# Macaron block with attention: key tiles scored in groups of four, values loaded on a semaphore of their own

## The chip, the cores and the metric

The kernel runs on one core of one Trainium2 chip. The metric is the time of one execution on the device in microseconds (us); lower is better. Engines are named as in the profile: PE is TensorE, PEld its weight loads, DVE is VectorE, ACT is ScalarE, POOL is GpSimd, SP is SyncE, which here only issues DMAs.

## The reference: what is computed

```python
x = x + 0.5 * ffn(layernorm(x), up, down, up_scale, down_scale, output_scale)
x = x + attention(layernorm(x), w_q, w_k, w_v, w_o)
x = x + 0.5 * ffn(layernorm(x), up, down, up_scale, down_scale, output_scale)

def attention(x, w_q, w_k, w_v, w_o):       # x: (2, 2048, 512), 16 heads of 32
    q, k, v = heads(x @ w_q.T), heads(x @ w_k.T), heads(x @ w_v.T)
    probs = softmax(q @ k.T / sqrt(32))
    return merge(probs @ v) @ w_o.T

def ffn(x, ...):                            # hidden size 2048, weights by their sign
    h = relu(x @ sign(up).T * up_scale)
    return h @ sign(down).T * down_scale * output_scale
```

Everything is float32. The attention part is what the change touches: two batches of 16 heads, 32 heads in all, each with 2048 queries and 2048 keys.

## The kernel before

The program has four stages: the first feed-forward part, the projections to queries, keys and values (stored in DRAM, queries and keys each as a rounded high part and a low part), the attention over 32 heads, and the output projection together with the second feed-forward part. Every engine has its instructions written out by hand in one order, and semaphores tie the engines together.

A head has 16 key tiles of 128 keys (`KT`) and four chunks of 512 queries (`QC`). One key tile with one chunk is called a **unit** here; a head has 64. For a unit, PE makes a block of scores, keys by queries, in one matmul with 98 rows (`scores`, L899 to L904: high and low parts stacked, and two rows that carry the negated maximum of each query). ACT takes the exponential of it into SBUF (L891). Three PSUM banks (`SR`) rotate for the scores, so the scores of a unit wait for the exponential three units earlier.

The maximum of each query has to be known before its scores are made, so beside each score block PE makes a block of queries by keys for a head later in time (`maxima`, L906 to L908; it runs four tiles ahead, `LEAD`), and DVE reduces that block to a maximum for each query (L836). Four banks (`MR`) rotate for these blocks. So PE's maxima of a unit wait until DVE has read the block four before it (`bank_free`, L962 to L974). In the last of the 32 heads, and the last four tiles of the one before, there are no maxima to make.

When all 64 maxima blocks of the next head are reduced, the **turn** follows: DVE negates them (L848), PE transposes the 128 by 16 result (L926), DVE splits it into a high and a low part (L854, L856), and SP writes both as two rows of the queries' tile (L769). The next head's first scores wait for these rows (`neg_loaded`, L979).

The probabilities of a key tile are multiplied by the values in `out_tile` (L928 to L943): four matmuls with 32 columns, one for each chunk, which use different columns of the array and run beside each other. POOL and DMAs with accumulation add the probabilities up for the softmax's denominator; PE finishes that with a matmul by ones (`sums`, L945 to L960) once a head. Eight tiles of probabilities (`PR`) rotate.

What sets PE's order in a head is `tensor_group` (L976 to L1003). A group is `G` = 2 key tiles. PE runs the eight units of the group, scores and maxima in turn, and then the outputs of the group before: `out_tile` for its two tiles. So a head has eight groups. The turn's transpose comes behind the group of tiles 12 and 13, the sums of the head before behind that of tiles 6 and 7, and ACT copies the head before's output out of its bank in the group of tiles 2 and 3 (L893).

SP, at the head's start, waits until PE has made all outputs of the head before (`head_free`, L772), and then issues in this order: the six loads of queries and keys for the head after next and the load of its values (L761, L763, seven DMAs on one semaphore), the four stores of the finished head (L297), the two moves of its sums (L302, L306), the two rows of maxima (L769) and the store of the inverse (L311).

Of the kernel before, what the change touches and what calls it, by code (L numbers as in the profile page):

```python
# [650 lines left out]

NB = 3
KQ, KM = 3 * HD, 3 * HD + 2
LEAD, G = 4, 2
NG = KT // G
PR = 8
SR, MR = 3, 4
UNITS = KT * QC
AHEAD = LEAD * QC
SUMS_AFTER = 3  # L660
SUMS_AT, TURN_AT = QC * G * (SUMS_AFTER + 1), QC * 7 * G
SLOTS = UNITS + 2
CHAINS = 2
PER = 7 * 16
TURN = KT - LEAD + 1
NEG = 3


def sums_after(H):

    return SUMS_AFTER if H < NH - 1 else SUMS_AFTER - 1


def chains_joined(H):
# [47 lines left out]
class Attention:  # L722
# [3 lines left out]
    def __init__(self, c, qk_parts, v_scr, head_out, ident, ones_sum):  # L726
        self.nc, self.qk_parts, self.v_scr, self.head_out, self.ident, self.ones_sum = c.nc, qk_parts, v_scr, head_out, ident, ones_sum
        self.q_st = [c.sb(f"att_q{i}", at, [P, SEQ], F32R) for i, at in enumerate((OUT_AT, HID_LO_AT, X0_AT))]
        self.k_st = [c.sb(f"att_k{i}", at, [P, SEQ], F32R) for i, at in enumerate((HID_HI_AT, INV_B_AT, RAW_AT))]
        self.v_st = [c.sb(f"att_v{i}", at, [P, KT, HD]) for i, at in enumerate((HID_AT + 2, HID_AT, INV_AT))]  # L730
        self.prob = [c.sb(f"att_p{i}", BIG_AT + 8 * i, [P, SEQ]) for i in range(PR)]
        self.acc = [c.sb(f"att_acc{i}", at, [P, SEQ]) for i, at in enumerate((CENT_AT, HI1_AT))]
        self.dma_acc = [[c.sb(f"att_dma_acc{i}_{x}", at, [P, SEQ]) for x, at in enumerate(ats)]
                        for i, ats in enumerate(((WORK_AT, SUM_AT), (LO1_AT, X1_AT)))]
        self.row_max = [c.sb(f"att_row_max{i}", HEAD_AT + 4 + 0.25 * i, [P, KT, QC]) for i in range(2)]
        self.neg_max = c.sb("att_neg_max", HEAD_AT + 4.5, [P, KT])
        self.neg_hi, self.neg_lo = c.sb("att_neg_hi", HEAD_AT + 5, [KT, P], F32R), c.sb("att_neg_lo", HEAD_AT + 5.5, [KT, P], F32R)
        self.m_ps, self.s_ps, self.o_ps = c.bank[0:4], c.bank[4:7], c.bank[7]
        self.loaded = [c.sem(f"att_loaded{i}") for i in range(NB)]
# [15 lines left out]


    def load(self, sp, X):
        b, row, col = X % NB, X % HEADS * HD, X // HEADS * SEQ
        for which, st in ((0, self.q_st[b]), (1, self.k_st[b])):
            for i, part in enumerate(((0, 0, 1), (0, 1, 0))[which]):  # L760
                sp.dma_start(f32(st[i * HD:(i + 1) * HD, :]),  # L761
                             self.qk_parts[which][part][row:row + HD, col:col + SEQ]).then_inc(self.loaded[b], 16)
        sp.dma_start(self.v_st[b][:], self.v_scr[col:col + SEQ, row:row + HD].rearrange("(t p) d -> p t d", p=P)  # L763
                     ).then_inc(self.loaded[b], 16)

    def max_rows(self, sp, H):
        for r, rows in enumerate((self.neg_hi, self.neg_lo)):
# [1 line left out]
            sp.dma_start(f32(self.q_st[H % NB][KQ + r:KQ + r + 1, :].rearrange("o (t p) -> o t p", p=P)),  # L769
                         f32(rows[:])).then_inc(self.neg_loaded, 16)  # L770

    def head_free(self, sp, H):  # L772

        sp.wait_ge(self.s_ready, UNITS * H)
        sp.wait_ge(self.p_used, KT * H)


# [79 lines left out]

    def vector_tile(self, dve, H, kt):
        T = H + 1 + (kt + LEAD) // KT
        for q in range(QC):  # L860
            p = QC * kt + q
            if T < NH:
                self.reduce_block(dve, UNITS * (H + 1) + AHEAD + p, self.m_ps[m_bank(H, slot(p))], T % 2, (kt + LEAD) % KT, q)
            if kt == TURN - 1 and q == 0 and H + 1 < NH:
                self.negate(dve, H + 1)
        if kt == TURN and H + 1 < NH:
            self.rows_out(dve, H + 1, self.turn_bank(H))
        if H > 0 and kt == (14 if H < NH - 1 else 12):
            self.head_out.invert(dve, H - 1)

# [12 lines left out]

    def scalar_tile(self, act, H, kt):
        self.tile_free(act, H, kt)
        if H > 0 and kt == G * (sums_after(H) + 1):
            act.wait_ge(self.t_ready, H)
            self.head_out.copy_sums(act, H - 1, self.sums_bank(H - 1))
        for q in range(QC):
            act.wait_ge(self.s_ready, UNITS * H + QC * kt + q + 1)  # L890
            self.nc.scalar.activation(self.prob[kt % PR][:, q * CH:(q + 1) * CH], self.s_ps[(UNITS * H + kt * QC + q) % SR][:], ACT.Exp,  # L891
                                      scale=SCALE).then_inc(self.exp_done, 1)
            if q == 1 and H > 0 and kt == G:  # L893
                act.wait_ge(self.p_used, KT * H)
                self.head_out.copy_out(act, H - 1, self.o_ps)

# [30 lines left out]

    def out_tile(self, pe, H, kt):  # L928
        pe.wait_ge(self.exp_done, UNITS * H + QC * (kt + 1))
        if kt == 0 and H > 0:  # L930
            pe.wait_ge(self.head_out.out_copied, H)
        for q in range(QC):
# [43 lines left out]
    def tensor_group(self, pe, H, u, beside=None):  # L976

        if u == 0:
            pe.wait_ge(self.neg_loaded, 32 * (H + 1))  # L979
            pe.wait_ge(self.ones_set, min(H + 1, NB))  # L980
        for kt in range(G * u, G * u + G):
            T = H + 1 + (kt + LEAD) // KT
            if kt == KT - LEAD and T < NH:
                pe.wait_ge(self.loaded[T % NB], PER * (T // NB + 1))
            for q in range(QC):
                self.scores(pe, H, kt, q)
                if T < NH:
                    at = slot(QC * kt + q)
                    self.bank_free(pe, H, at)
                    self.maxima(self.m_ps[m_bank(H, at)], T, (kt + LEAD) % KT, q)  # L990
                if beside:
                    beside(QC * (kt - G * u) + q)
        if G * u <= TURN < G * u + G and H + 1 < NH:
            self.bank_free(pe, H, TURN_SLOT)
            self.transpose_max(pe, H + 1, self.turn_bank(H))
        for kt in range(G * u - G, G * u):
            if kt >= 0:
                self.out_tile(pe, H, kt)
            elif H > 0:
                self.out_tile(pe, H - 1, KT + kt)  # L1000
        if u == sums_after(H) and H > 0:
            self.bank_free(pe, H, SUMS_SLOT)
            self.sums(pe, H - 1)  # L1003
# [8 lines left out]
FIRST_TURN = (NCH - 1, 6)  # L1012
FOUR_FROM = FIRST_FROM[NCH - 1, 0]


def macaron_kernel(nc, xT, w_qT, w_kT, w_vT, w_oT, upT, downT, up_scale, down_scale, output_scale, outT):
    ctx = ExitStack()
    with ctx:
# [40 lines left out]
        with nc.Block() as block:  # L1059
            @block.sync  # L1060
            def _(sp):
# [23 lines left out]
                for n in range(NCH):  # L1085
# [3 lines left out]
                    for t in range(NT):  # L1089
                        qkv.store(sp, n, t)  # L1090
                        if n == 4 and t == 2:
                            qkv.all_stored(sp, 4)
                            sp.wait_ge(att.ones_set, 2)
                            att.load(sp, 0)
                        if n == 4 and t == 6:
                            att.load(sp, 1)
                        if (n, t) == FIRST_TURN:
                            att.max_rows(sp, 0)
                qkv.all_stored(sp, NCH)

                for H in range(NH):
                    if H > 0:
                        att.head_free(sp, H)
                    if H + 2 < NH:
                        att.load(sp, H + 2)
                    if H == 0:
                        sp.dma_start(wo_raw[:], w_oT).then_inc(wo_loaded, 16)
                    if H == LAST - 1:
# [196 lines left out]
            def _(pe):  # L1305
# [23 lines left out]
                pe.wait_ge(qkv.qk_read, 8 * NCH)  # L1329
                pe.wait_ge(qkv.v_read, 4 * NCH)  # L1330
                for H in range(NH):
                    for u in range(NG):
                        def beside(i):
                            t = u + 1 if H == LAST else 0
                            first = (H, u, i) == (LAST - 1, NG - 1, 0)
                            if first:
# [4 lines left out]
                            if (H, u) == (LAST - 1, NG - 1) or (H == LAST and u < 3):  # L1341
                                oproj.product(pe, 0, t, range(STEPS * i // 8, STEPS * (i + 1) // 8))
# [6 lines left out]
                for kt in range(KT - G, KT):  # L1349
                    att.out_tile(pe, LAST, kt)  # L1350
                att.sums(pe, LAST)

# [41 lines left out]
```

## Time and profile before

| what | value |
|---|---|
| time of the kernel before, median of 3 runs | 2979.45 us (2978.91 to 2981.06) |
| the profiled execution's own time | 2976.84 us |
| its span on the core | 2975.0 us |
| mean granted TensorE clock | 0.994 |
| PE busy | 2898.6 us, 97% of the span |
| DVE busy | 2051.4 us, 69% |
| ACT busy | 1603.5 us, 54% |
| POOL busy | 1383.1 us, 46% |
| attention: first and last score matmul | 817.9 and 2404.6 us |

The profiled execution lies inside the program's usual time: 1.84 us lie around its span, and it is 2.61 us below the median of the three runs. The attention takes 1587 us of the span, more than half. The times of the rows below are microseconds from the start of the span.

### The profile page before, as it was taken

What the parts mean: (1) busy time and instruction counts of PE and PEld (TensorE: products, weight loads), DVE (VectorE), ACT (ScalarE), POOL (GpSimd) and SP (SyncE); (2) the same over time, 40 slices, a digit from 0 to 9 for tenths busy, and PEclk for the clock granted to TensorE, in tenths of its full rate; (3) what the DMA queues carried; (4) which work ended last, traced back from release to release, by engine and by line L of the source; (5) the groups of instructions that cost most, each with busy time, mean ns of one, the idle gap of its engine ahead of it and who ended that gap; (6) DMA issues with size and microseconds to landing.
All of it is one profiled execution on the core that took longest, in us unless ns stands there. A gap on an engine that the chain in (4) does not pass through costs nothing.

```text
span 2975.0 us, 38468 instructions
## 1 busy us (share of the span) xinstructions
PE 2898.6 (97%) x14528; PEld 1939.1 (65%) x14528; DVE 2051.4 (69%) x3050; ACT 1603.5 (54%) x2851; POOL 1383.1 (46%) x522
## 2 busy tenths in 40 slices
PE   6999998999999999999999999999999899999999
PEld 5888887887755555555555555555555457888887
DVE  5555555767787787878787878788888355555553
ACT  5444434332276666666666666666666553343333
POOL 0000000000089898988898889898888720000000
PEclk9999999999999999999999999999999999999999
DMA  4110002555389999998999999999898872222200
GB/s 154 59 57 29 29 29 62 199 192 177 124 219 205 220 209 224 203 231 198 228 203 233 200 229 202 229 204 229 204 229 207 220 196 69 57 57 57 57 29 29
DMA packets 189275, 459.97 MB, mean 155 GB/s; under 512 B 90273, under 2 KB 91297, under 8 KB 148769
## 3 DMA queue, kind: packets, MB, share of 16 engines
q0 software_dynamic: 36720, 267.40, 39.0%
q1 hardware_dynamic: 152368, 190.11, 22.6%
q8 instruction: 114, 1.87, 0.3%
q14 instruction: 73, 0.59, 0.1%
HBM read 121.91 MB, written 67.63 MB: 64 GB/s over the span
## 4 chain that ended last, share of the span: by engine, by line
PE 88%; DVE 4%; DMA 3%; ACT 3%; POOL 1%; issue 1%; SPq 0%; ACTq 0%; DVEq 0%; POOLq 0%
PE bank L903 16%; PE bank L511 16%; PE bank L530 15%; PE bank L934 15%; PE bank L907 14%; PE bank L642 8%; PE bank L382 3%; ACT att_p L891 2%; DMA att_q<-att_neg_lo 1%; DVE att_row_max L836 1%; PE bank L958 1%; PE bank L950 1%; DVE norm_inv L109 1%; DVE norm_work L119 1%; POOL att_acc L792 1%
## 5 line engine op out<-in xcount | busy, mean ns | idle before, releaser
L836 DVE TENSOR_REDUCE att_row_max<-bank 128x1 f32<-128x512 f32 x2048 | 1255.2, 681 | 318.0 <-PE bank L907 318.0
L891 ACT ACTIVATE att_p<-bank 128x512 f32<-128x512 f32 x2048 | 1035.5, 627 | 414.3 <-PE bank L903 408.5
L792 POOL TENSOR_TENSOR att_acc<-att_acc,att_p 128x2048 f32<-128x2048 f32 x217 | 1066.6, 4915 | 32.8 <-ACT att_p L891 28.2
L903 PE MATMUL bank<-att_q,att_k 98*128 98x512 f32 x2048 | 848.5, 415 | 18.2 <-ACT att_p L891 11.2
L907 PE MATMUL bank<-att_k,att_q 96*128 96x512 f32 x2048 | 808.1, 396 | 10.8 <-DVE att_row_max L836 10.6
L903 PEld LDWEIGHTS bank<-att_q,att_k 98*128 98x128 f32 x2048 | 384.4, 188 | 396.7 <-issue 202.4
L934 PE MATMUL bank<-att_p,att_v 128*32 128x512 f32 x4096 | 497.1, 603 | 0.0
L443 DVE TENSOR_TENSOR ffn_hid_lo<-ffn_hid,ffn_hid_hi 128x512 fp32r<-128x512 f32 x256 | 176.0, 688 | 420.8 <-ACT ffn_hid_hi L486 402.5
L483 ACT ACTIVATE ffn_hid<-bank,up_s 128x512 f32<-128x512 f32 x256 | 176.1, 688 | 488.0 <-PE bank L511 487.2
L907 PEld LDWEIGHTS bank<-att_k,att_q 96*128 96x128 f32 x2048 | 389.6, 190 | 60.6 <-DVE att_row_max L836 13.3
L511 PE MATMUL bank<-hi,ffn_up_w 128*128 128x512 f32 x1024 | 401.0, 392 | 13.6 <-DVE lo L123 13.6
L530 PE MATMUL bank<-ffn_hid_hi,ffn_down_w 128*128 128x512 f32 x1024 | 399.6, 390 | 1.9 <-DVE ffn_hid_lo L443 1.9
L511 PE MATMUL bank<-lo,ffn_up_w 128*128 128x512 f32 x1024 | 400.7, 391 | 0.0
L530 PE MATMUL bank<-ffn_hid_lo,ffn_down_w 128*128 128x512 f32 x1024 | 399.7, 390 | 0.0
L780 POOL MEMSET att_k<- 2x2048 f32 x3 | 5.4, 1805 | 814.8 <-PE bank L530 501.7
L807 POOL DMA_DIRECT2D att_dma_acc<-att_p x161 | 203.8, 1266 | 139.4 <-DMA att_dma_acc<-att_p 97.8
L934 PEld LDWEIGHTS bank<-att_p,att_v 128*32 128x32 f32 x4096 | 107.5, 109 | 242.8 <-ACT att_p L891 158.5
L511 PEld LDWEIGHTS bank<-hi,ffn_up_w 128*128 128x128 f32 x1024 | 193.6, 189 | 56.1 <-issue 15.2
L530 PEld LDWEIGHTS bank<-ffn_hid_hi,ffn_down_w 128*128 128x128 f32 x1024 | 192.7, 188 | 42.9 <-DVE ffn_hid_lo L443 2.4
L511 PEld LDWEIGHTS bank<-lo,ffn_up_w 128*128 128x128 f32 x1024 | 193.6, 189 | 40.8
L530 PEld LDWEIGHTS bank<-ffn_hid_lo,ffn_down_w 128*128 128x128 f32 x1024 | 192.7, 188 | 40.5
L486 ACT ACTIVATE ffn_hid_hi<-bank,up_s 128x512 fp32r<-128x512 f32 x256 | 174.6, 682 | 0.0
(104 smaller groups left out, 2236.8 us busy)
## 6 DMA issues: line engine op xcount, KB each, us to landing
att_dma_acc<-att_p POOLq DMA_DIRECT2D x225, 1024.0 KB, 8.9
att_dma_acc<-att_dma_acc POOLq DMA_DIRECT2D x30, 1024.0 KB, 12.6
x<-x_after_ffn SPq DMA_DIRECT2D x16, 1024.0 KB, 7.6
att_q<-q_hi SPq DMA_DIRECT2D x64, 256.0 KB, 4.0
att_k<-k_hi SPq DMA_DIRECT2D x64, 256.0 KB, 10.0
x_after_ffn<-x_out SPq DMA_DIRECT2D x8, 1024.0 KB, 9.4
q_hi<-qkv_o_hi SPq DMA_DIRECT2D x32, 256.0 KB, 2.0
q_lo<-qkv_o_lo SPq DMA_DIRECT2D x32, 256.0 KB, 2.4
```

Source lines behind the costliest of these rows:

```text
L443: nc.vector.tensor_tensor(self.hid_lo[:, ht % RING, :], self.hid[:, ht % RAW, :], f32(self.hid_hi[:, ht % RING, :]), ALU.subtract).then_in ...
L483: nc.scalar.activation(self.hid[:, ht % RAW, :], self.up_ps[ht % 2][:], ACT.Relu, scale=self.vecs["up"][:, ht:ht + 1])
L511: ins = nc.tensor.matmul(self.up_ps[ht % 2][:], signs.up[:, ht // 4, dt, ht % 4 * P:(ht % 4 + 1) * P], part[N % 2][:, dt, :], start=(dt == ...
L530: ins = nc.tensor.matmul(self.down_ps[dt][:], signs.down[:, h, dt * P:(dt + 1) * P], part[:, h % RING, :], start=(h == 0 and i == 0), stop ...
L642: ins = self.nc.tensor.matmul(self.out_ps[t % QR][:], left, right, start=(dt == 0 and (a, b) == (0, 0)), stop=(dt == DT - 1 and (a, b) == ...
L792: self.nc.gpsimd.tensor_tensor(self.acc[H % 2][:], a[:], self.prob[kt % PR][:], ALU.add).then_inc(self.summed, 1)
L807: self.nc.gpsimd.dma_start(into[:], self.prob[kt % PR][:], accum_op=ALU.add).then_inc(self.dma_summed[x], 16)
L836: self.nc.vector.tensor_reduce(self.row_max[odd][:, qt, q:q + 1], m[:], axis=AX.X, op=ALU.max).then_inc(self.m_read, 1)
L891: self.nc.scalar.activation(self.prob[kt % PR][:, q * CH:(q + 1) * CH], self.s_ps[(UNITS * H + kt * QC + q) % SR][:], ACT.Exp, scale=SCALE ...
L903: self.nc.tensor.matmul(self.s_ps[i % SR][:], self.k_st[H % NB][0:KM, kt * P:(kt + 1) * P], self.q_st[H % NB][0:KM, q * CH:(q + 1) * CH], ...
L907: self.nc.tensor.matmul(m[:], self.q_st[T % NB][0:KQ, qt * P:(qt + 1) * P], self.k_st[T % NB][0:KQ, q * CH:(q + 1) * CH], start=True, stop ...
L934: ins = self.nc.tensor.matmul(self.o_ps[rows, :], self.v_st[H % NB][:, kt, :], self.prob[kt % PR][:, q * CH:(q + 1) * CH], start=(kt == 0) ...
```

## The change

Tiles are grouped by four instead of by two in all heads but the last (`GROUPS`), which keeps pairs (`PAIRS`). So PE makes 16 units of scores and maxima in a row and then the outputs of the four tiles of the group before. The sums come behind the group of tiles 4 to 7. The turn comes behind the outputs that follow the group of tiles 8 to 11, since with a lead of four tiles the next head's maxima are complete there; DVE negates and splits ahead of its reductions of tile 12. ACT copies the head before's output in tile 4. Values have a semaphore of their own, `v_loaded`, which the first output of a head waits for. SP loads queries and keys as soon as all scores of the head before are made, and values once all its outputs are made.

```diff
-LEAD, G = 4, 2
-NG = KT // G
+LEAD = 4
+GROUPS = tuple(tuple(range(kt, kt + 4)) for kt in range(0, KT, 4))
+PAIRS = tuple((kt, kt + 1) for kt in range(0, KT, 2))
+SUMS_GROUP, TURN_GROUP = 1, 2
-SUMS_AT, TURN_AT = QC * G * (SUMS_AFTER + 1), QC * 7 * G
+SUMS_AT, TURN_AT = QC * GROUPS[SUMS_GROUP + 1][0], QC * (KT - LEAD)
-PER = 7 * 16
+PER = 6 * 16
+def groups(H):
+    return GROUPS if H < NH - 1 else PAIRS
...
+    def load_values(self, sp, X):
+        b, row, col = X % NB, X % HEADS * HD, X // HEADS * SEQ
         sp.dma_start(self.v_st[b][:], self.v_scr[col:col + SEQ, row:row + HD].rearrange("(t p) d -> p t d", p=P)
-                     ).then_inc(self.loaded[b], 16)
+                     ).then_inc(self.v_loaded[b], 16)
...
-    def head_free(self, sp, H):
+    def scores_made(self, sp, H):
         sp.wait_ge(self.s_ready, UNITS * H)
+    def outputs_made(self, sp, H):
         sp.wait_ge(self.p_used, KT * H)
...
     def vector_tile(self, dve, H, kt):
+        if kt == KT - LEAD and H + 1 < NH:
+            self.negate(dve, H + 1)
+            self.rows_out(dve, H + 1, self.turn_bank(H))
...
-            if kt == TURN - 1 and q == 0 and H + 1 < NH:
-                self.negate(dve, H + 1)
-        if kt == TURN and H + 1 < NH:
-            self.rows_out(dve, H + 1, self.turn_bank(H))
...
-            if q == 1 and H > 0 and kt == G:
+            if q == 1 and H > 0 and kt == groups(H)[1][0]:
                 act.wait_ge(self.p_used, KT * H)
                 self.head_out.copy_out(act, H - 1, self.o_ps)
...
     def out_tile(self, pe, H, kt):
         pe.wait_ge(self.exp_done, UNITS * H + QC * (kt + 1))
+        if kt == 0:
+            pe.wait_ge(self.v_loaded[H % NB], 16 * (H // NB + 1))
...
-        for kt in range(G * u, G * u + G):
+        first = groups(H)[u][0]
+        for kt in groups(H)[u]:
...
-        if G * u <= TURN < G * u + G and H + 1 < NH:
+        if u > 0:
+            for kt in groups(H)[u - 1]:
+                self.out_tile(pe, H, kt)
+        elif H > 0:
+            for kt in groups(H - 1)[-1]:
+                self.out_tile(pe, H - 1, kt)
+        if u == TURN_GROUP and H + 1 < NH:
             self.bank_free(pe, H, TURN_SLOT)
             self.transpose_max(pe, H + 1, self.turn_bank(H))
-        for kt in range(G * u - G, G * u):
-            if kt >= 0:
-                self.out_tile(pe, H, kt)
-            elif H > 0:
-                self.out_tile(pe, H - 1, KT + kt)
...
                 for H in range(NH):
                     if H > 0:
-                        att.head_free(sp, H)
+                        att.scores_made(sp, H)
                     if H + 2 < NH:
                         att.load(sp, H + 2)
+                    if H > 0:
+                        att.outputs_made(sp, H)
+                    if H + 2 < NH:
+                        att.load_values(sp, H + 2)
```

How the instructions stand, at the places on which the prediction rests. First PE, at the end of the first stretch of scores (L903, and L914 in the changed kernel) and maxima (L907, and L918) of the attention's first head; L934 and L947 are the outputs. Before, 32 such matmuls, those of 16 units, run ahead of the first outputs, since the first group of the first head has no outputs behind it:

```order
L903 MATMUL bank<-att_q_84,att_k_87 128x512 [waits att_exp_done]
L907 MATMUL bank<-att_k_88,att_q_85 128x512 [waits att_m_read]
L934 MATMUL bank<-att_p_93,att_v_90 32x512 [waits att_exp_done]
L934 MATMUL bank<-att_p_93,att_v_90 32x512 x3
L934 MATMUL bank<-att_p_94,att_v_90 32x512 [waits att_exp_done]
L934 MATMUL bank<-att_p_94,att_v_90 32x512 x3
L903 MATMUL bank<-att_q_84,att_k_87 128x512 [waits att_exp_done]
```

And now at the same place, ahead of which 32 units run in this first head (16 in all later groups):

```order
L914 MATMUL bank<-att_q_84,att_k_87 128x512 [waits att_exp_done]
L918 MATMUL bank<-att_k_88,att_q_85 128x512 [waits att_m_read]
L947 MATMUL bank<-att_p_93,att_v_90 32x512 [waits att_v_loaded0,att_exp_done]
L947 MATMUL bank<-att_p_93,att_v_90 32x512 x3
L947 MATMUL bank<-att_p_94,att_v_90 32x512 [waits att_exp_done]
L947 MATMUL bank<-att_p_94,att_v_90 32x512 x3
L947 MATMUL bank<-att_p_95,att_v_90 32x512 [waits att_exp_done]
L947 MATMUL bank<-att_p_95,att_v_90 32x512 x3
L947 MATMUL bank<-att_p_96,att_v_90 32x512 [waits att_exp_done]
L947 MATMUL bank<-att_p_96,att_v_90 32x512 x3
L914 MATMUL bank<-att_q_84,att_k_87 128x512 [waits att_exp_done]
```

The outputs of four tiles now stand together, and the waits on `att_m_read` (DVE's reading of a maxima block) and `att_exp_done` are the same ones on twice as long a stretch.

DVE over the end of one head in the middle of the attention, before; `att_row_max` is where the reductions go, `head_inv_t` the inverse of the head before's sums:

```order
L836 TENSOR_REDUCE att_row_max_107<-bank 128x1 [waits att_m_ready]
L848 TENSOR_REDUCE att_neg_max<-att_row_max_108 128x16 [waits att_neg_pe,att_m_read]
L836 TENSOR_REDUCE att_row_max_107<-bank 128x1 [waits att_m_ready] x7
L854 CAST att_neg_hi<-bank 16x128 [waits att_neg_loaded,att_neg_pe]
L856 TENSOR_TENSOR att_neg_lo<-bank,att_neg_hi 16x128 [waits att_neg_dve]
L836 TENSOR_REDUCE att_row_max_107<-bank 128x1 [waits att_m_ready] x4
L318 RECIPROCAL head_inv_t<-head_tot_t 128x16 [waits head_inv_stored,head_sums_moved]
```

And now:

```order
L848 TENSOR_REDUCE att_row_max_108<-bank 128x1 [waits att_m_ready] x52
L860 TENSOR_REDUCE att_neg_max<-att_row_max_108 128x16 [waits att_neg_pe,att_m_read]
L866 CAST att_neg_hi<-bank 16x128 [waits att_neg_loaded,att_neg_pe]
L868 TENSOR_TENSOR att_neg_lo<-bank,att_neg_hi 16x128 [waits att_neg_dve]
L848 TENSOR_REDUCE att_row_max_107<-bank 128x1 [waits att_m_ready] x12
L318 RECIPROCAL head_inv_t<-head_tot_t 128x16 [waits head_inv_stored,head_sums_moved]
```

The negation and the split have moved ahead of the reductions of tiles 12 to 15, and DVE now waits there for PE's transpose with no reduction in between.

SP at the start of a head, before:

```order
L761 DMA att_q_84<-q_hi 32x2048 [waits att_p_used,att_s_ready]
L761 DMA att_q_84<-q_hi 32x2048
L761 DMA att_q_84<-q_lo 32x2048
L761 DMA att_k_87<-k_hi 32x2048
L761 DMA att_k_87<-k_lo 32x2048
L761 DMA att_k_87<-k_hi 32x2048
L763 DMA att_v_90<-v_rows 128x16x32
L297 DMA attention_out<-head_raw 32x512 [waits head_out_copied]
```

And now:

```order
L767 DMA att_q_84<-q_hi 32x2048 [waits att_s_ready]
L767 DMA att_q_84<-q_hi 32x2048
L767 DMA att_q_84<-q_lo 32x2048
L767 DMA att_k_87<-k_hi 32x2048
L767 DMA att_k_87<-k_lo 32x2048
L767 DMA att_k_87<-k_hi 32x2048
L772 DMA att_v_90<-v_rows 128x16x32 [waits att_p_used]
L297 DMA attention_out<-head_raw 32x512 [waits head_out_copied]
```

The order of the DMAs is the same; the wait for the outputs (`att_p_used`) has moved from the first load to the load of the values.

## Rows read from the trace of the kernel before

**Rows 1.** The page: the chain that ended last, shares of the span by engine

```profile
PE 88%; DVE 4%; DMA 3%; ACT 3%; POOL 1%; issue 1%; SPq 0%; ACTq 0%; DVEq 0%; POOLq 0%
```

**Rows 2.** Busy time in 200 us of the attention (us, busy of each engine, clock, DMA)

```profile
1420.00:1620.00 200.00, 199.03 (x1116) 108.17 (x1116) 162.06 (x278) 135.00 (x269) 175.28 (x65) 1.00 0.93 216
```

**Rows 3.** The chain in order of time, one head (start us, us, what)

```profile
1551.25 1.85 PE bank L934 x16
...
1557.05 1.85 PE bank L934 x16
...
1563.28 1.85 PE bank L934 x16
...
1576.73 0.86 PE bank L950 x8
1577.59 0.86 PE bank L958 x8
...
1594.11 0.28 PE bank L926
...
1600.18 1.85 PE bank L934 x16
```

**Rows 4.** PE's timeline over one group (start, us, line, what [idle before <-releaser])

```profile
1503.85 0.50 PE L903 MATMUL bank<-att_q,att_k 98*128 98x512 f32 x1 [0.32 <-DMA att_q<-att_neg_lo]
1504.19 0.40 PE L907 MATMUL bank<-att_k,att_q 96*128 96x512 f32 x1
...
1507.47 0.40 PE L907 MATMUL bank<-att_k,att_q 96*128 96x512 f32 x1
1507.80 1.92 PE L934 MATMUL bank<-att_p,att_v 128*32 128x512 f32 x16
1509.65 0.50 PE L903 MATMUL bank<-att_q,att_k 98*128 98x512 f32 x1
```

**Rows 5.** DVE's timeline, same head

```profile
1504.63 4.88 DVE L836 TENSOR_REDUCE att_row_max<-bank 128x1 f32<-128x512 f32 x8 [1.21 <-PE bank L907]
...
1550.41 0.24 DVE L318 RECIPROCAL head_inv_t<-head_tot_t 128x16 f32<-128x16 f32 x1
```

**Rows 6.** The page: the reductions (xcount | busy, mean ns | idle before)

```profile
L836 DVE TENSOR_REDUCE att_row_max<-bank 128x1 f32<-128x512 f32 x2048 | 1255.2, 681 | 318.0 <-PE bank L907 318.0
```

**Rows 7.** The timeline of the first head's first 16 units

```profile
817.51 10.96 DVE L836 TENSOR_REDUCE att_row_max<-bank 128x1 f32<-128x512 f32 x18 [0.57 <-PE bank L907]
...
817.98 0.47 PE L903 MATMUL bank<-att_q,att_k 98*128 98x512 f32 x1 [0.27 <-issue]
...
819.19 7.95 ACT L891 ACTIVATE att_p<-bank 128x512 f32<-128x512 f32 x16
...
826.13 0.19 PEld L907 LDWEIGHTS bank<-att_k,att_q 96*128 96x128 f32 x1 [0.23 <-DVE att_row_max L836]
...
826.56 1.92 PE L934 MATMUL bank<-att_p,att_v 128*32 128x512 f32 x16
```

**Rows 8.** PE's waits from 820 to 2405 us (total, times, longest)

```profile
PE bank L903 <- DMA att_q<-att_neg_lo: 2.9, 5, 1.0
```

**Rows 9.** SP's timeline (start, us, what)

```profile
1512.52 0.42 SPq L763 DMA_DIRECT2D att_v<-v_rows  x1
1512.99 15.29 SPq L297 DMA_DIRECT2D attention_out<-head_raw  x4
1530.33 0.55 SPq L302 DMA_DIRECT2D prob_sums<-head_total  x1
1535.70 0.34 SPq L306 DMA_DIRECT2D head_tot_t<-prob_sums  x1
...
1547.70 1.38 SPq L769 DMA_DIRECT2D att_q<-att_neg_lo  x1
```

**Rows 10.** ACT's timeline in the second to last head

```profile
2326.42 1.91 ACT L366 ACTIVATE hi<-op_raw 128x2048 fp32r<-128x2048 f32 x1 [4.59 <-POOL op_raw L353]
```

**Rows 11.** The chain in order of time, between the last two heads

```profile
2353.99 1.12 SPq L344
```

More of the change, by code:

```diff
@@ L659 @@
 AHEAD = LEAD * QC
-SUMS_AFTER = 3
-SUMS_AT, TURN_AT = QC * G * (SUMS_AFTER + 1), QC * 7 * G
+SUMS_AT, TURN_AT = QC * GROUPS[SUMS_GROUP + 1][0], QC * (KT - LEAD)
 SLOTS = UNITS + 2
 CHAINS = 2
-PER = 7 * 16
-TURN = KT - LEAD + 1
+PER = 6 * 16
 NEG = 3
+def groups(H):
+    return GROUPS if H < NH - 1 else PAIRS
 def sums_after(H):
-    return SUMS_AFTER if H < NH - 1 else SUMS_AFTER - 1
+    return SUMS_GROUP if H < NH - 1 else 2
 def chains_joined(H):
@@ L738, in __init__ @@
         self.m_ps, self.s_ps, self.o_ps = c.bank[0:4], c.bank[4:7], c.bank[7]
-        self.loaded = [c.sem(f"att_loaded{i}") for i in range(NB)]
+        self.loaded, self.v_loaded = [c.sem(f"att_loaded{i}") for i in range(NB)], [c.sem(f"att_v_loaded{i}") for i in range(NB)]
         self.ones_set = c.sem("att_ones_set")
@@ L885, in scalar_tile @@
         self.tile_free(act, H, kt)
-        if H > 0 and kt == G * (sums_after(H) + 1):
+        if H > 0 and kt == groups(H)[sums_after(H) + 1][0]:
             act.wait_ge(self.t_ready, H)
@@ L991, in tensor_group @@
                 if beside:
-                    beside(QC * (kt - G * u) + q)
-        if G * u <= TURN < G * u + G and H + 1 < NH:
+                    beside(QC * (kt - first) + q)
+        if u > 0:
[5 more added lines that the diff above has]
+        if u == TURN_GROUP and H + 1 < NH:
             self.bank_free(pe, H, TURN_SLOT)
             self.transpose_max(pe, H + 1, self.turn_bank(H))
-        for kt in range(G * u - G, G * u):
-            if kt >= 0:
-                self.out_tile(pe, H, kt)
-            elif H > 0:
-                self.out_tile(pe, H - 1, KT + kt)
         if u == sums_after(H) and H > 0:
@@ L1012 @@
 FIRST_TURN = (NCH - 1, 6)
+FILL_FROM = QC * len(GROUPS[-1]) - 8
 FOUR_FROM = FIRST_FROM[NCH - 1, 0]
@@ L1094, in _ @@
                             att.load(sp, 0)
+                            att.load_values(sp, 0)
                         if n == 4 and t == 6:
                             att.load(sp, 1)
+                            att.load_values(sp, 1)
                         if (n, t) == FIRST_TURN:
@@ L1331, in _ @@
                 for H in range(NH):
-                    for u in range(NG):
+                    for u in range(len(groups(H))):
                         def beside(i):
                             t = u + 1 if H == LAST else 0
-                            first = (H, u, i) == (LAST - 1, NG - 1, 0)
-                            if first:
+                            ahead = (H, u) == (LAST - 1, len(GROUPS) - 1) and i >= FILL_FROM
+                            if ahead and i == FILL_FROM:
                                 pe.wait_ge(att.m_read, UNITS * NH)
@@ L1340, in beside @@
                                 pe.wait_ge(att.neg_dve, NEG * NH)
-                            if (H, u) == (LAST - 1, NG - 1) or (H == LAST and u < 3):
-                                oproj.product(pe, 0, t, range(STEPS * i // 8, STEPS * (i + 1) // 8))
+                            if ahead or (H == LAST and u < 3):
+                                j = i - FILL_FROM if ahead else i
+                                oproj.product(pe, 0, t, range(STEPS * j // 8, STEPS * (j + 1) // 8))
                             if (H, u, i) == (LAST, 3, 7):
@@ L1348, in _ @@
                         att.tensor_group(pe, H, u, beside)
-                for kt in range(KT - G, KT):
+                for kt in PAIRS[-1]:
                     att.out_tile(pe, LAST, kt)
```

## The prediction

> **What bounds the kernel now.** I read the chain by engine first: 88% of it is PE [rows 1]. Then a stretch in the middle of the attention: in 200 us PE is busy 199.03, at the full clock, while DVE has 162.06, ACT 135.00 and POOL 175.28 [rows 2]. So a head lasts as long as PE's instructions, and the question is what PE's own order costs. The chain over one head gives that: from the outputs of one head's first group to those of the next, 1551.25 to 1600.18, are 48.93 us [rows 3]. A plain group of two tiles lasts 5.80 (1551.25 to 1557.05). The head has eight of them, 46.40; ACT's copy of the finished head makes one of them 6.23 (to 1563.28), 0.43 more; the sums are twice 0.86; the transpose of the turn is 0.28. That makes 48.83, and 0.10 is left over.
>
> Inside a group, count from its first score, 1503.85 [rows 4]. The first maxima follow at 0.34, the eighth at 3.62 (1507.47), so 14 steps of 0.234 lie between, and a unit of scores and maxima takes 0.468. The outputs start 0.33 later, at 3.95, and 16 of them take 1.85, until 5.80.
>
> DVE needs longer for a unit than PE. It starts 0.78 after the first score (1504.63) and takes 4.88 for eight reductions [rows 5]; one lasts 0.68 [rows 6], so they start (4.88 - 0.68) / 7 = 0.60 apart. In each unit DVE falls back 0.13, and it catches up while PE makes outputs, which need nothing of it. That is the heart of this case.
>
> **Groups of four.** Maxima of unit n take the bank of unit n - 4, so they start at the earliest when DVE has finished that one: 0.78 + 0.60 (n - 4) + 0.68, and a handover. For n = 7, the last of a group now, this is 3.26 against the 3.62 at which PE is there anyway: no wait. With 16 units PE would be at the last maxima at 0.34 + 30 x 0.234 = 7.36, but DVE has finished unit 11 only at 0.78 + 11 x 0.60 + 0.68 = 8.06.
>
> The trace of before holds this stretch once: the first head's first group has no outputs behind it, so 16 units run in a row there [rows 7]. DVE's 18 reductions are two left over and these 16, (10.96 - 0.68) / 17 = 0.605 apart. The one for unit 11 is the 14th and ends at 817.51 + 13 x 0.605 + 0.68 = 826.05; the weight load of the last maxima comes at 826.13 and is put down to DVE. The handover is 0.08, and the outputs come 0.43 behind it, not 0.33. From the first score to the outputs it is 826.56 - 817.98 = 8.58; my reckoning gives 8.06 + 0.08 + 0.43 = 8.57. ACT paces the start of this stretch, (7.95 - 0.60) / 15 = 0.49 for a unit, but not its end.
>
> So a group of four takes 8.57 + 32 outputs at 1.85 / 16, 3.70, together 12.27, against 2 x 5.80 = 11.60: 0.67 more. Without DVE it would be 7.36 + 0.33 + 3.70 = 11.39, 0.21 less than now, since one change from outputs to scores and back is saved (0.34 and 0.33 where a step is 0.234) [rows 4].
>
> The Trainium skill (VectorE: DVE Perf Modes, the section on the TRN2 errata) gives a VectorE instruction that reads PSUM 120 cycles and one for each element at 0.96 GHz, which for 512 is 0.66 us. That is near the 0.68 of one instruction, but the starts here are 0.60 apart; taken as the pace it would put the last maxima at 8.78 and the forecast some 75 us higher. The measurement decides.
>
> **The head's other pieces.** ACT's copy moves to tile 4, the start of the second group. It still holds up a few scores, but DVE has started by then and its pace sets the group's end: even with the copy's 0.49, ACT finishes unit 12 at about 0.6 + 12 x 0.49 + 0.49 + 0.6 = 7.6, before 8.06. So its 0.43 goes, and the 0.10 too. Sums and transpose stay, 1.72 and 0.28; the negation is done while PE makes the 3.70 of outputs ahead of the transpose, and the split (two instructions of 0.28 or so) fits into the 0.78 that DVE stands anyway. The head becomes 4 x 12.27 + 2.00 = 51.08, so 51.08 - 48.93 = 2.15 more. If the copy isn't hidden it is 2.58; if the hold is 0.1 less in each group, 1.75.
>
> 29 heads (the second to the thirtieth): 29 x 2.15 = +62.4. The first head: 32 units now run in a row, 0.78 + 27 x 0.60 + 0.68 + 0.08 + 0.43 = 18.2, then 3.7, then 12.27 and 12.55: 46.7; before 8.58 + 1.85 + 6 x 5.80 + 0.28 = 45.5. That is +1.2. The last head keeps pairs.
>
> The thirty-first head has a hold of its own: ACT stands 4.59 until POOL has scaled the first chunk of the output projection, at 2326.42 [rows 10]. POOL's place from the head's start stays, so the first two groups' extra goes into that wait. But PE comes out of it with four tiles' outputs more still to make (tiles 4 to 7 stand behind the third group now), 3.7, less about 0.5 for the changes between outputs and scores saved after it: +3.2. From there the end follows, since SP's loads for the projection wait for the last outputs of this head, at 2353.99 [rows 11]. Bounds 0 and 5.
>
> **The turn.** The transpose now has 0.28 + 8.57 + 3.70 = 12.6 us ahead of the next head's first score; before it was 1594.11 to 1600.18 + 1.85, 7.9 [rows 3]. The rows of maxima were late by up to 1.0, in all 2.9 us of PE [rows 8]; at one head it is the 0.32 in rows 4. SP's issue at 1547.70 [rows 9] comes 43.9 into the head; now it can be at about 40 of 51. That wait goes: -2.9, at most.
>
> **Loads.** Queries and keys are issued about 6 to 10 us sooner, values about 3.6 later (12.3 into the head, where the outputs end, against 1512.52 - 1503.85 = 8.7). Neither was waited for; both have a head or more: nothing. What is queued behind the values on SP is the point: the four stores took 15.29 behind them, then the sums move out at 1530.33, 26.5 into the head, and in again at 1535.70, 31.9 [rows 9]. DVE wants them at 1550.41, 46.6 [rows 5]. Now the stores end about 28.1 into the head, so the sums come 1.7 later, at 33.6, and DVE wants them at 46.8: 13 us for a small transfer. Nothing, but it is rival three. POOL and the DMA engines (0.93 busy [rows 2]) get the same work in a longer head.
>
> **The sum.** 62.4 + 1.2 + 3.2 - 2.9 = +63.9 on the profiled execution's 2976.84 gives 3040.7; the median of the runs lies 2.6 above that execution, so 3043.3.
>
> **Rivals.** *Fewer switches win (faster).* If DVE didn't hold PE in the second half of a group, a head would be 4 x 11.39 + 0.43 + 2.00 + 0.10 = 48.1, 0.85 less, and with the turn's 2.9 the time would be 2979.45 - 30 x 0.85 - 2.9 = 2951. For it: DVE has 318 us of idle time in its reductions [rows 6], so on average it keeps up. Against it: it is held to four banks, and rows 7 show the wait. It decides if DVE's pace came to 0.53 or less. The Trainium skill (TensorEngine Tiling (Array Packing), Key Properties) says that changing the tiling mode drains the TensorE, and outputs with 32 columns are another mode than scores; the trace agrees, at 0.1 us a switch. By that rule alone this change is a gain. Chance 4%.
>
> *The hold is half as large*, because what saves PE elsewhere in a long stretch doesn't show in the first head, where ACT paced the start: a group of 11.39 + 0.44 = 11.83, a head 4 x 11.83 + 2.00 = 49.32, +0.39, time 2979.45 + 29 x 0.39 + 1.2 + 3.2 - 2.9 = 2992. Against it: the formula doesn't use ACT's pace and meets 8.58. Chance 8%; and 2% that it all cancels.
>
> *SP's queue becomes a wait (much slower).* If the sums of the head before land more than 13 us after their issue, DVE stands at L318 with tile 15's reductions behind it, and PE behind those. Each us late costs 29; 2 us late gives about 3100. For it: DMAs are dense and the stores already took 15 us. Against it: 13 us are left. Chance 8%.
>
> **How the numbers follow.** The forecast has 78%. Its own range is 0.4 us for a head either way, the two bounds of a head above, 12 in all, and 0 to 5 for the tail: 3028 to 3057. Towards the half-sized hold I go down to 3024, and to 3058 above; it leaves out about 20%. What a measurement of this kernel can tell from no change is 0.2%, 6 us. Faster 4%, same 2%, slower 94%.
>
> **What would show it.** Right: a head of 51 us in the chain; weight loads of the maxima (now L918) held by DVE late in each group, about 0.8 us a group; DVE's reductions in runs of 16 of about 9.7; no wait for the rows of maxima; ACT's copy costing PE nothing by the group's end. Wrong: groups of 11.4 (rival one), or DVE idle at L318 (rival three). A head of 51 with another total would mean the tail is mis-sized.

## The result and the profile after

| | before | changed |
|---|---|---|
| median of 4 runs | 2979.18 us (2977.14 to 2981.06) | 3011.73 us (3009.84 to 3016.62) |
| ratio to before, 95% interval | | 1.0108 (1.0096 to 1.0120) |
| span of the profiled execution | 2975.0 us | 3008.0 us |
| one head in the middle | 48.93 us | 50.15 us |

The change makes the kernel slower by 1.1%, 32.6 us. I had forecast slower, by 64. The direction and its mechanism were right, the loss that I forecast was twice the one measured, and the time lies under my range.

The chain of the changed kernel in order of time over one head (start us, us, what), which answers to [rows 3]:

```profile
1502.19 3.57 PE bank L947 x32
1505.76 0.21 PE bank L937
...
1514.33 3.57 PE bank L947 x32
...
1526.42 3.57 PE bank L947 x32
...
1538.53 3.57 PE bank L947 x32
1542.10 0.86 PE bank L963 x8
1542.96 0.86 PE bank L971 x8
...
1552.34 3.57 PE bank L947 x32
```

From 1502.19 to 1552.34 are 50.15 us. The outputs of four tiles take 3.57, not twice 1.85. A plain group's scores run from 1517.90 (1514.33 + 3.57) to 1526.42, 8.52. The group with the transpose (L937) lasts from 1505.76 to 1514.33, 8.57: the transpose costs 0.04 or so, where it stood in the chain with 0.28 before [rows 3].

PE and its weight loads near the end of a group of four (timeline, [idle before <-releaser]):

```profile
1550.64 0.19 PEld L918 LDWEIGHTS bank<-att_k,att_q 96*128 96x128 f32 x1 [0.30 <-DVE att_row_max L848]
1550.65 0.50 PE L918 MATMUL bank<-att_k,att_q 96*128 96x512 f32 x1
1550.75 0.19 PEld L914 LDWEIGHTS bank<-att_q,att_k 98*128 98x128 f32 x1
1550.98 0.39 PE L914 MATMUL bank<-att_q,att_k 98*128 98x512 f32 x1
1551.24 0.19 PEld L918 LDWEIGHTS bank<-att_k,att_q 96*128 96x128 f32 x1 [0.30 <-DVE att_row_max L848]
...
1551.84 0.19 PEld L918 LDWEIGHTS bank<-att_k,att_q 96*128 96x128 f32 x1 [0.30 <-DVE att_row_max L848]
...
1552.27 0.16 PEld L947 LDWEIGHTS bank<-att_p,att_v 128*32 128x32 f32 x8 [0.24 <-ACT att_p L902]
```

Each maxima block's weight load is released by DVE, 0.60 apart: that is DVE's pace, not PE's 0.47. PE itself has no gap in these rows: the next scores start 0.33 behind the held maxima (1550.98), where a step was 0.234 before, and still inside its 0.50. So the hold shows in PEld's waits and not in PE's busy time. DVE, for the same kernel, now reduces 16 blocks without a gap and then stands:

```profile
1518.60 9.66 DVE L848 TENSOR_REDUCE att_row_max<-bank 128x1 f32<-128x512 f32 x16 [2.33 <-PE bank L918]
1530.70 9.66 DVE L848 TENSOR_REDUCE att_row_max<-bank 128x1 f32<-128x512 f32 x16 [2.44 <-PE bank L918]
```

And the waits of the attention (us in total, times, longest). The first was forecast; before, DVE held a weight load of a maxima block once in the whole attention, the one at 826.13 in [rows 7]. The last, the sign of rival three, came once and was short. The rows of maxima, waited for in [rows 8], are in the list no more:

```profile
PEld bank L918 <- DVE att_row_max L848: 161.6, 579, 0.3
...
DVE head_inv_t L318 <- DMA head_tot_t<-prob_sums: 0.2, 1, 0.2
```

579 is close to 30 heads with four groups of five held loads.

### The profile page after: what moved, and what is told of

Its sections match the earlier page's. It is cut to its first block, busy times and chain, and to the rows that moved or that the text cites. A ratio compares the mean times of both kernels' runs of the same rounds, so it can differ in the third digit from the quotient of the medians.

```text
span 3008.0 us, 38440 instructions
## 1 busy us (share of the span) xinstructions
PE 2938.1 (98%) x14528; PEld 1910.1 (64%) x14528; DVE 2043.4 (68%) x3050; ACT 1615.0 (54%) x2851; POOL 1378.6 (46%) x522
## 4 chain that ended last, share of the span: by engine, by line
PE 92%; DVE 3%; ACT 3%; DMA 1%; issue 1%; POOL 0%; ACTq 0%; SPq 0%; DVEq 0%; POOLq 0%
PE bank L918 17%; PE bank L914 16%; PE bank L511 15%; PE bank L947 15%; PE bank L530 15%; PE bank L642 7%; PE bank L382 3%; ACT att_p L902 2%; PE bank L971 1%; PE bank L963 1%; DMA att_dma_acc<-att_p 1%; DVE norm_inv L109 1%; ACT head_raw L286 0%; DVE norm_work L119 0%; PE bank L176 0%
## 5 line engine op out<-in xcount | busy, mean ns | idle before, releaser
L848 DVE TENSOR_REDUCE att_row_max<-bank 128x1 f32<-128x512 f32 x2048 | 1240.6, 677 | 305.0 <-PE bank L918 305.0
L902 ACT ACTIVATE att_p<-bank 128x512 f32<-128x512 f32 x2048 | 1047.1, 654 | 383.9 <-PE bank L914 370.9
L804 POOL TENSOR_TENSOR att_acc<-att_acc,att_p 128x2048 f32<-128x2048 f32 x217 | 1022.6, 4712 | 220.8 <-ACT att_p L902 216.5
L918 PE MATMUL bank<-att_k,att_q 96*128 96x512 f32 x2048 | 876.0, 429 | 11.0 <-DVE att_row_max L848 11.0
L914 PE MATMUL bank<-att_q,att_k 98*128 98x512 f32 x2048 | 842.4, 413 | 15.5 <-ACT att_p L902 11.7
L914 PEld LDWEIGHTS bank<-att_q,att_k 98*128 98x128 f32 x2048 | 385.5, 188 | 274.1 <-ACT att_p L902 130.8
L918 PEld LDWEIGHTS bank<-att_k,att_q 96*128 96x128 f32 x2048 | 387.2, 189 | 212.4 <-DVE att_row_max L848 175.1
L947 PE MATMUL bank<-att_p,att_v 128*32 128x512 f32 x4096 | 473.8, 602 | 0.0
L947 PEld LDWEIGHTS bank<-att_p,att_v 128*32 128x32 f32 x4096 | 120.6, 110 | 265.5 <-issue 208.1
L819 POOL DMA_DIRECT2D att_dma_acc<-att_p x161 | 160.1, 994 | 18.5 <-DMA att_dma_acc<-att_p 13.1
```

Of the source, the lines that this page charges most:

```text
L804: self.nc.gpsimd.tensor_tensor(self.acc[H % 2][:], a[:], self.prob[kt % PR][:], ALU.add).then_inc(self.summed, 1)
L848: self.nc.vector.tensor_reduce(self.row_max[odd][:, qt, q:q + 1], m[:], axis=AX.X, op=ALU.max).then_inc(self.m_read, 1)
L914: self.nc.tensor.matmul(self.s_ps[i % SR][:], self.k_st[H % NB][0:KM, kt * P:(kt + 1) * P], self.q_st[H % NB][0:KM, q * CH:(q + 1) * CH], ...
L918: self.nc.tensor.matmul(m[:], self.q_st[T % NB][0:KQ, qt * P:(qt + 1) * P], self.k_st[T % NB][0:KQ, q * CH:(q + 1) * CH], start=True, stop ...
L947: ins = self.nc.tensor.matmul(self.o_ps[rows, :], self.v_st[H % NB][:, kt, :], self.prob[kt % PR][:, q * CH:(q + 1) * CH], start=(kt == 0) ...
```

## The experiments

All ratios are to the kernel before, run on the same chip; the medians of before were 2977.4 to 2980.5, by the chip, so two rows are compared by their ratios. The halved reductions leave out half of each block of maxima, so those two kernels are no candidates. "A head" is the distance of two heads' first scores in the middle of the attention.

| kernel | median us | ratio, 95% interval | a head, us |
|---|---|---|---|
| before | 2979 | 1 | 48.93 |
| changed | 3011.73 | 1.0108 (1.0096 to 1.0120) | 50.15 |
| groups of four, halved reductions | 2944.15 | 0.9886 (0.9865 to 0.9908) | 47.88 |
| before, halved reductions | 2966.04 | 0.9966 (0.9953 to 0.9980) | 48.76 |
| pairs with the rest of the change | 2980.04 | 1.0000 (0.9991 to 1.0009) | 48.98 |
| groups of four, loads as before | 3032.69 | 1.0186 (1.0171 to 1.0202) | 50.1 to 55.0 |
| groups of four, copy first | 3012.60 | 1.0106 (1.0091 to 1.0121) | 50.17 |
| before, copy first | 2971.07 | 0.9963 (0.9951 to 0.9975) | 48.6 |
| groups of 3, 3, 2, 2, 2, 2, 2 | 2981.88 | 1.0004 (0.9996 to 1.0013) | 49.10 |
| before, transpose behind the outputs | 2972.83 | 0.9983 (0.9974 to 0.9993) | 48.65 |
| pairs, rest of the change, copy first | 2965.21 | 0.9948 (0.9936 to 0.9960) | 48.65 |
| the same, transpose between scores | 2965.71 | 0.9959 (0.9946 to 0.9972) | 48.59 |
| the same, transpose behind tiles 12 and 13's group | 2958.87 | 0.9931 (0.9917 to 0.9944) | 48.29 |

**Is it DVE that holds a group of four?** Two kernels with DVE's work halved, one in fours and one in pairs:

```diff
-self.nc.vector.tensor_reduce(self.row_max[odd][:, qt, q:q + 1], m[:], axis=AX.X, op=ALU.max)
+self.nc.vector.tensor_reduce(self.row_max[odd][:, qt, q:q + 1], m[:, 0:CH // 2], axis=AX.X, op=ALU.max)
-                                      scale=SCALE)
+                                      scale=SCALE * 0.1)
```

> The changed kernel, but DVE's reductions (L848) read only the first 256 of each maxima block's 512 columns, and the exponential's argument is scaled by a further 0.1 so that it stays finite; half of each row of the maxima is left out. Theory (DVE's pace holds PE in the second half of a group of four): with reductions some 0.33 us apart nothing holds, a group is 7.36 + 0.33 + 3.57 = 11.26 instead of 12.10, ACT's copy costs its 0.43 again, so a head is 4 x 11.26 + 1.72 + 0.03 + 0.43 = 47.2 to 47.5 us instead of 50.14, and the time about 3012 - 30 x 2.8 = 2928 (2920 to 2938). Rival (a group of four is held by something else, ACT's exponentials or PE's own weight loads): the head stays at 49.5 to 50.1 and the time over 2995.

> The kernel before with the same halved reductions and the same scale. Theory: in groups of two DVE never held PE, so the head stays at 48.9 and the time at 2979 within 4 us. Rival: if DVE bounds the kernel before as well, by the average, it falls by more than 10 us.

The chain of the first, one head from 1503.79 to 1551.66:

```profile
1503.79 3.57 PE bank L947 x32
1507.36 0.86 PE bank L963 x8
1508.21 0.86 PE bank L971 x8
...
1517.02 3.57 PE bank L947 x32
1520.59 0.21 PE bank L937
...
1528.40 3.57 PE bank L947 x32
...
1539.78 3.57 PE bank L947 x32
1544.98 0.49 ACT head_raw L286
...
1551.66 3.57 PE bank L947 x32
```

A plain group now lasts 1539.78 - 1528.40 = 11.38 instead of 12.10, and the group with ACT's copy 11.88, so the copy costs its 0.5 again. The head falls from 50.15 to 47.88. It is 0.4 to 0.7 above what I expected, and the time lies 6 us above my range: ACT's exponentials, 0.49 apart, hold the scores where DVE did. Still, the rival's 49.5 to 50.1 is ruled out: it was DVE that held the group.

Pairs fall by 0.17 a head, where I expected nothing, and by 13 us in all. About 3 us of the 13 lie ahead of the attention, in the first reductions, and some in the rows of maxima, which were late less. The 0.17 is at the transpose. In the kernel before, its weight load waits for DVE once in every head, 30 times in all:

```profile
1594.11 0.09 PEld L926 LDWEIGHTS bank<-ident,att_neg_max 128*16 128x16 f32 x1 [0.41 <-DVE att_row_max L836]
```

With halved reductions this wait is gone, and the group with the transpose lasts 1537.34 - 1531.43 = 5.91, 0.11 more than a plain one:

```profile
1531.43 1.85 PE bank L934 x16
...
1537.34 1.85 PE bank L934 x16
...
1543.14 1.85 PE bank L934 x16
```

So of the 0.28 before, only 0.11 is the transpose; 0.17 is a wait for DVE. DVE's pace costs groups of four 2.3 us a head and pairs 0.17. Without it, fours would beat pairs by 0.88. That this is so close to the 0.85 of my first rival is in part luck: its outputs and its transpose were too dear, and it had no hold by ACT.

**Is it the group size alone?**

```diff
-GROUPS = tuple(tuple(range(kt, kt + 4)) for kt in range(0, KT, 4))
-SUMS_GROUP, TURN_GROUP = 1, 2
+GROUPS = PAIRS
+SUMS_GROUP, TURN_GROUP = 3, 5
```

> The changed kernel with groups of two in every head, and all else of the change: the loads' new order, the values' own semaphore, the turn's transpose behind the outputs that follow tiles 10 and 11. Theory: the group size alone makes the change slower; here the transpose costs 0.03 to 0.2 instead of 0.28 (DVE's negation is just not ready when the outputs end) and no head waits for its rows of maxima: 30 x 0.1 to 0.25 plus 3, so 2969 to 2974. Rival (the new order of loads or of the turn costs something): 2979 or more.

Time and head are those of before. So the group size carries all of the loss. The gain that I expected, 5 to 10 us, isn't there; the timeline shows a part of why:

```profile
1542.43 0.22 DVE L860 TENSOR_REDUCE att_neg_max<-att_row_max 128x16 f32<-128x64 f32 x1
1542.76 0.09 PEld L937 LDWEIGHTS bank<-ident,att_neg_max 128*16 128x16 f32 x1 [1.05 <-DVE att_row_max L848]
1542.79 0.27 PE L937 MATMUL bank<-ident,att_neg_max 128*16 128x128 f32 x1 [0.18 <-DVE att_neg_max L860]
```

In pairs the outputs are over before DVE has negated, and PE waits for it at every turn; the group with the turn lasts 0.34 more than a plain one, against 0.30 before. (The 0.37 in later expectations is this 0.34.) In fours the 3.57 of outputs cover the negation. The second head takes back another 1.7 us (52.32 between its first scores and the third's, against 50.66 before); I didn't take that apart.

**What are the loads worth?** Groups of four, with the order of SP as before:

```diff
                         att.scores_made(sp, H)
+                        att.outputs_made(sp, H)
                     if H + 2 < NH:
                         att.load(sp, H + 2)
-                    if H > 0:
-                        att.outputs_made(sp, H)
```

> The changed kernel with SP waiting for scores and outputs of the head before ahead of all seven loads, as before; groups of four stay. Theory: the loads' order isn't on the path; 3012 within 4 us. Rival (the early loads of queries and keys delay other transfers, or gain something): a difference of more than 6 us.

The theory fell: 21 us slower. My third rival happens here, in another form: I had feared that the sums land more than 13 us after their issue; here they take 5.7 (965.35 to 971.07), and the issue itself is late. SP's timeline and DVE's at one of the two slowest heads:

```profile
935.68 0.44 SPq L772 DMA_DIRECT2D att_v<-v_rows  x1
936.16 23.50 SPq L297 DMA_DIRECT2D attention_out<-head_raw  x4
959.70 1.21 SPq L302 DMA_DIRECT2D prob_sums<-head_total  x1
...
965.35 0.33 SPq L306 DMA_DIRECT2D head_tot_t<-prob_sums  x1
```

```profile
955.32 7.25 DVE L848 TENSOR_REDUCE att_row_max<-bank 128x1 f32<-128x512 f32 x12
971.07 0.25 DVE L318 RECIPROCAL head_inv_t<-head_tot_t 128x16 f32<-128x16 f32 x1 [8.51 <-DMA head_tot_t<-prob_sums]
971.24 5.62 DVE L848 TENSOR_REDUCE att_row_max<-bank 128x1 f32<-128x512 f32 x9
```

All seven loads and then the four stores stand in SP's queue, and the stores take 23.50 us to issue. The sums come too late, DVE stands 8.51 at the inverse with reductions behind it, and PE stands behind those. At some twenty other heads DVE's wait is 1.5 to 3.4. The rows of maxima stand behind the sums in SP's queue as well, and at four heads PE waits for them. In the whole attention:

```profile
DVE head_inv_t L318 <- DMA head_tot_t<-prob_sums: 67.7, 22, 8.6
...
PE bank L914 <- DMA att_q<-att_neg_lo: 12.5, 4, 4.8
```

In the changed kernel, with queries and keys issued ahead and the values by themselves, the stores of a head in the middle take 7.07 (they took 15.29 in [rows 9]), and the sums go out before they are late:

```profile
1530.06 0.38 SPq L772 DMA_DIRECT2D att_v<-v_rows  x1
1532.14 7.07 SPq L297 DMA_DIRECT2D attention_out<-head_raw  x4
1544.64 0.55 SPq L302 DMA_DIRECT2D prob_sums<-head_total  x1
```

So the change has two parts that belong together: groups of four delay the point at which all of a head's outputs are made, and with the old order of loads that would cost 21 us more. In pairs all the rest of the change together, loads and turn, is worth nothing in time; no run parts the two, though the stores take less there too (3.6 to 5.1 a head).

**Is ACT's copy hidden in fours, and what is it worth in pairs?**

```diff
+        if H > 0 and kt == groups(H)[1][0]:
+            act.wait_ge(self.p_used, KT * H)
+            self.head_out.copy_out(act, H - 1, self.o_ps)
         for q in range(QC):
...
-            if q == 1 and H > 0 and kt == groups(H)[1][0]:
-                act.wait_ge(self.p_used, KT * H)
-                self.head_out.copy_out(act, H - 1, self.o_ps)
```

> The changed kernel with ACT's copy of the finished head's output ahead of the first exponential of tile 4 instead of behind the second. In groups of four I took the copy to be hidden by DVE's pace. If so, this changes nothing: 3012 within 4 us, head 50.1. Rival (the copy still costs PE about 0.4 a head): about 12 us less.

> The kernel before with ACT's copy ahead of the first exponential of tile 2, where ACT stands idle for 1.8 us, instead of behind the second. In groups of two the copy costs PE 0.43 a head; here it should cost 0.05 to 0.15: 30 x 0.3 to 0.38 less, 2966 to 2971. Rival (the wait for the last outputs comes too late, and the exponentials start later by the copy's whole length): no change or slower.

Both as expected, the second at the upper edge of its range. In fours nothing changes, since DVE's pace sets the group's end. In pairs a head falls by 0.33 and the time by 0.4%: the copy now lies in ACT's idle time.

**Does the formula hold for another size?**

```diff
-GROUPS = tuple(tuple(range(kt, kt + 4)) for kt in range(0, KT, 4))
-SUMS_GROUP, TURN_GROUP = 1, 2
+GROUPS = ((0, 1, 2), (3, 4, 5), (6, 7)) + tuple((kt, kt + 1) for kt in range(8, KT, 2))
+SUMS_GROUP, TURN_GROUP = 2, 4
```

> The changed kernel with groups of 3, 3, 2, 2, 2, 2, 2 tiles in all heads but the last. The formula for the hold gives a group of three 0.78 + 7 x 0.60 + 0.68 + 0.08 = 5.74 at its last maxima, against 5.49 without a hold, and the whole group 5.74 + 0.43 + 2.71 = 8.88. Without a hold it would be 8.53. So the first two groups take 17.8 to 17.9 against 4 x 5.80 x 3 / 4 = 17.4 in pairs; the time is 2 to 6 us above that of the same kernel in pairs. Rival (the hold is not by DVE's pace against four banks, but comes only in long groups): groups of 8.5 and a time some 10 us below that of pairs.

The chain of that kernel (the first group of three starts at 1506.42 + 1.85):

```profile
1506.42 1.85 PE bank L947 x16
...
1514.41 1.85 PE bank L947 x16
1517.90 0.49 ACT head_raw L286
...
1522.62 2.71 PE bank L947 x24
...
1529.52 2.71 PE bank L947 x24
```

The first group's scores take 1514.41 - 1508.27 = 6.14; the formula says 5.74 + 0.43 = 6.17, and 5.82 without a hold. The second group's take 6.36 (1516.26 to 1522.62): ACT's copy, in the chain there, isn't hidden in a group of three. The outputs take the 2.71 worked out. The head is 49.10, 0.12 above the same in pairs, which would be 3.5 us in all; the ratios, 1.0004 and 1.0000, don't tell the two kernels apart. The rival's 10 us less is ruled out.

**What does the transpose cost, and which kernel beats both?** The kernel before with the transpose moved:

```diff
-        if G * u <= TURN < G * u + G and H + 1 < NH:
-            self.bank_free(pe, H, TURN_SLOT)
-            self.transpose_max(pe, H + 1, self.turn_bank(H))
         for kt in range(G * u - G, G * u):
...
+        if G * u <= TURN < G * u + G and H + 1 < NH:
+            self.bank_free(pe, H, TURN_SLOT)
+            self.transpose_max(pe, H + 1, self.turn_bank(H))
```

> The kernel before with the transpose behind the outputs that follow tiles 12 and 13, not ahead of them. It tells what the transpose itself costs: theory, 0.03 there instead of 0.28, as in the changed kernel's groups. But the rows of maxima then start 1.9 us later and were late by up to 1.0 already: PE should wait some 1 to 2.5 us at each head's start, and the time rise by 25 to 65 us. Rival (the transpose costs 0.28 wherever it stands, and the rows have slack): 2979 within 4 us.

```profile
1585.49 1.85 PE bank L934 x16
...
1591.29 1.85 PE bank L934 x16
1593.14 0.21 PE bank L926
...
1597.12 1.85 PE bank L934 x16
```

From 1591.29 to 1597.12 are 5.83, so the transpose costs 0.03 there; a head falls by 0.28. Its weight load still waits for DVE, but while PE makes outputs. My fear for the rows was wrong: PE waits for them at nine heads instead of five, 5.3 us in all, and the time falls by 0.2% instead of rising by 25 us or more.

Then three versions in pairs. The first is pairs with the rest of the change and ACT's copy first:

> The changed kernel with groups of two in every head and ACT's copy ahead of the first exponential of tile 2. If the two effects add, the copy's 9 to 12 us come off the time of groups of two with the rest of the change: 2958 to 2965, faster than both kernels. Rival (with the copy gone, DVE or POOL holds): 2968 or more.

It came just past the edge of the theory, 2965.21: the copy brings its gain of 0.33 a head, and the rest of the change in pairs brings none to a head in the middle (48.65, against 48.6 with the copy alone). The second moves its transpose between the scores of tiles 12 and 13 (`if kt == KT - LEAD` inside the loop over tiles), the third behind the outputs that follow tiles 12 and 13 (its edit, against the first):

```diff
-SUMS_GROUP, TURN_GROUP = 3, 5
-SUMS_AT, TURN_AT = QC * GROUPS[SUMS_GROUP + 1][0], QC * (KT - LEAD)
+SUMS_GROUP, TURN_GROUP = 3, 6
+SUMS_AT, TURN_AT = QC * GROUPS[SUMS_GROUP + 1][0], QC * GROUPS[TURN_GROUP + 1][0]
...
             self.negate(dve, H + 1)
+        if kt == GROUPS[TURN_GROUP + 1][0] and H + 1 < NH:
             self.rows_out(dve, H + 1, self.turn_bank(H))
```

> The changed kernel with groups of two, ACT's copy first, and the turn's transpose behind the scores of tile 12 instead of behind the outputs that follow tiles 10 and 11, where PE waited about 0.3 a head for DVE's negation. By then DVE has negated. Theory: the 0.37 that the turn costs there falls to 0.05 to 0.28, a head of 48.65 becomes 48.3 to 48.55, and the time 2955 to 2962. Rival (the transpose between scores costs as much as a wait): 2965.

> The changed kernel with groups of two, ACT's copy first, and the transpose behind the outputs that follow tiles 12 and 13. There DVE has long negated and the transpose costs 0.03, so a head of 48.65 us (transpose behind tiles 10 and 11's group, 0.37) becomes 48.3; the rows of maxima are late at a few heads by up to 1 us, as in the kernel before with its transpose moved behind the outputs. Theory: 2955 to 2961. Rival (what the turn saves is lost to late rows): 2964 or more.

The second missed: a head fell by 0.06 only and the time not at all; the turn's group still costs 0.3 more than a plain one. Its timeline shows where: the transpose takes 0.12 between scores, and behind it three weight loads of maxima wait 0.19, 0.30 and 0.20, two for DVE's reductions and one for its split. The third came out as expected, a head of 48.29 and 2958.87 us, 0.7% faster than the kernel before and the fastest that computes the whole result.

## Why the prediction was wrong in size

Its steps, one by one, on the spans (+33.0 measured, +63.9 forecast):

- **DVE holds PE in the second half of a group: right.** A group's scores took 8.52 to 8.54 against 8.57, and the held loads are there. The difference is 0.16 of the head's 0.93 too much. (One figure beside the sum is wrong: starts 0.66 apart would put the last maxima at 0.78 + 11 x 0.66 + 0.68 = 8.72, not 8.78; nothing hangs on it.)
- **Outputs of four tiles at 32 x 1.85 / 16: the step that failed.** 1.85 holds a fixed part. Eight sums' matmuls of the same form, behind outputs, take 0.86 [rows 3], so 16 are 1.72, and 0.13 is paid once for a run of them between scores, of 16 or of 32: 3.57, not 3.70. I had the saving of a switch in the scores' part and scaled it away in the outputs'. Four groups make 0.52 a head, 15 us.
- **The transpose stays at 0.28: failed.** I took a piece of the chain for the instruction's own cost, though 0.17 of it was the wait for DVE, as the halved reductions in pairs show. Behind outputs and ahead of scores it is 0.03: 0.25 a head, 7 us. The kernel before with the transpose moved shows it alone. Why the remaining 0.11 falls to 0.03 there is open.
- **ACT's copy is hidden: right,** by the run with the copy first. **No head waits for the rows of maxima: right.**
- Together a head is 50.15 and not 51.08. From the second head's first score to the thirty-first's the trace has 1424.4 before and 1456.7 after, +32.3: 29 x 1.22 = 35.4, less the 2.9 of the rows. I had 62.4 - 2.9 = 59.5.
- **The first head** was +0.4, not +1.2, mostly for the same two reasons. **The thirty-first** was +1.9, and all behind it -1.1, where I had +3.2. The rest, ahead of the attention, is -0.6.
- **The loads are worth nothing:** wrong in this kernel, though it didn't enter the sum: they are what keeps the third rival away. The stores that I carried over at 15.29 took 7.07.

My range took 0.4 a head either way for the terms that I knew to be open, DVE's hold and the copy. Both were right. The error sat in two terms that I took as given, and both made the forecast too high.

## What to carry to other kernels

A long run of one kind of work is only free as far as the buffers between two engines reach: with four banks and a consumer 0.13 us a unit slower, PE could run eight units ahead without a wait and lost 0.7 to 0.8 us in sixteen, though the consumer was idle a fifth of the time. Before a duration is scaled to twice as many instructions, split it into a fixed and a running part by two rows of different count. And before a piece of the chain is taken as an instruction's own cost, look in its weight load for a wait: moved behind other work, the same instruction can be nearly free.

## What the runs showed of the hardware

- A run of 32-column matmuls between full-width scores costs 0.107 us each (0.86 for 8) and 0.13 once: 1.85 for 16, 2.71 for 24, 3.57 for 32. The Trainium skill (TensorEngine Tiling (Array Packing), Key Properties) says that a change of tiling mode drains the TensorE. The rows agree that a change costs time and give its size; that the time is a drain, none of them shows.
- SP's time to issue four stores of 64 KB was 5.9 to 7.7 us a head with only the values' load right ahead of them, and with all seven loads ahead 8.0 to 17.0 in the kernel before and 7.2 to 24.6 in groups of four (the first 29 heads of each trace). What is queued behind such an issue is late by as much. What in the queue holds the issue, no run here shows.
